# A two-layer vision tower: softmax sums carried by every feature row, a two-part output projection, and row numbers copied by another engine

## The reference, cut to what matters

```
x    = layernorm(h)
q    = rope(x @ Wq) / 4;  kv = rope(x @ Wkv);  v = layernorm per head of kv, * g + b
o    = softmax(q kv^T) v             per image and head; rows 0..997 attend to 0..997,
                                     the last 32 rows to all 1030
h    = h + o_ctx @ Wo_ctx + bo_ctx   for rows 0..997
h    = h + o_lat @ Wo_lat + bo_lat   for the last 32 rows
h    = h + sum over the two best experts of share * swiglu(x_expert)
```

## Time and profile before

| | us |
|---|---|
| median of the timed runs | 4640.12 |
| lowest and highest of 3 | 4629.51, 4647.07 |
| the profiled execution's own time | 4654.99 |
| its span, first to last instruction | 4653.2 |
| stretch of attend | 2178.0 to 3446.6 |
| stretch of project | 3446.6 to 3693.7 |
| stretch of mixture | 4027.2 to 4622.0 |

### The profile page before, as it was taken

The page is one execution under the profiler, slowest core; times in us unless marked ns, Lnnn a source line. Parts: engine busy times, 40 slices in busy tenths (PEclk is TensorE's granted clock), DMA queues, the critical chain, the costliest instruction groups (busy, mean ns, idle before and its releaser), DMA issues. The chain is left out here.

```text
span 4653.2 us, 74405 instructions
## 1 busy us (share of the span) xinstructions
PE 3991.2 (86%) x24046; PEld 2485.3 (53%) x24046; DVE 2531.1 (54%) x4411; ACT 1439.1 (31%) x2890; POOL 1191.6 (26%) x1370
## 2 busy tenths in 40 slices
PE   8799777689999997664999999999957589898885
PEld 8688555557666665442233333333327566666664
DVE  1476369923222222786877777777824454444442
ACT  0122110011111111342577777777741111111110
POOL 0222010034444442464000000000013100177775
PEclk9899897789999998675899999999987699999998
DMA  6122111032333332345233224323239411377776
GB/s 207 49 65 54 40 38 28 25 75 59 61 61 69 70 63 45 105 128 134 42 56 61 47 47 66 50 47 51 48 81 239 106 30 47 88 165 159 162 160 148
DMA packets 335639, 381.02 MB, mean 82 GB/s; under 512 B 44708, under 2 KB 292035, under 8 KB 333823
## 3 DMA queue, kind: packets, MB, share of 16 engines
q1 hardware_dynamic: 255903, 289.46, 25.8%
q0 software_dynamic: 57856, 69.18, 8.7%
q10 hardware_dynamic: 21728, 20.14, 1.5%
HBM read 261.04 MB, written 123.33 MB: 83 GB/s over the span
## 5 line engine op out<-in xcount | busy, mean ns | idle before, releaser
L1931 DVE TENSOR_REDUCE at_mx<-psum 128x1 f32<-128x998 f32 (+1 forms) x768 | 886.4, 1192 | 264.1 <-PE psum L1756 263.5
L1886 ACT ACTIVATE at_p<-psum 128x512 f32<-128x512 f32 (+3 forms) x1536 | 851.5, 588 | 300.1 <-PE psum L1830 270.1
L1830 PE MATMUL psum<-at_q,at_k 99*128 99x512 bf16 (+3 forms) x1536 | 522.1, 383 | 20.3 <-issue 15.2
L1756 PE MATMUL psum<-at_k,at_q 96*128 96x512 bf16 (+3 forms) x1536 | 475.6, 392 | 66.7 <-DMA at_k<-qk_parts 29.3
L1816 PE MATMUL psum<-at_p,at_v 128*32 128x486 f32 (+3 forms) x3072 | 408.3, 604 | 1.0 <-ACT at_p L1886 0.7
L1830 PEld LDWEIGHTS psum<-at_q,at_k 99*128 99x128 bf16 (+1 forms) x1536 | 155.5, 102 | 426.6 <-ACT at_p L1886 273.3
L1173 DVE TENSOR_TENSOR ex_hT<-ex_silu,psum 128x384 f32<-128x384 f32 (+1 forms) x288 | 147.4, 512 | 416.2 <-ACT ex_silu L1142 271.0
L1142 ACT ACTIVATE ex_silu<-psum 128x384 f32<-128x384 f32 (+1 forms) x288 | 131.5, 457 | 776.5 <-PE psum L1086 646.2
L1736 POOL DMA_DIRECT2D o_parts<-at_o x24 | 12.9, 539 | 1247.9 <-DVE at_mx L1931 900.9
L1108 PE MATMUL psum<-ex_wd,ex_hT 128*128 128x192 f32 (+1 forms) x1728 | 291.5, 327 | 0.0
L1756 PEld LDWEIGHTS psum<-at_k,at_q 96*128 96x128 bf16 (+1 forms) x1536 | 152.4, 105 | 229.4 <-DVE at_mx L1931 64.0
(11 more groups left out here) (361 smaller groups left out, 6846.2 us busy)
## 6 DMA issues: line engine op xcount, KB each, us to landing
mx_wd<-in_e_dT SPq DMA_DIRECT2D x72, 288.0 KB, 3.9
qk_parts<-hd_parts SPq DMA_DIRECT2D x32, 579.4 KB, 3.8
at_k<-qk_parts SPq DMA_DIRECT2D x144, 128.8 KB
at_q<-qk_parts SPq DMA_DIRECT2D x144, 124.8 KB
tok_p<-in_x SPq DMA_DIRECT2D x12, 1176.0 KB
mx_wg<-in_e_gT SPq DMA_DIRECT2D x72, 192.0 KB, 2.4
mx_wu<-in_e_uT SPq DMA_DIRECT2D x72, 192.0 KB, 3.4
o_parts<-at_o POOLq DMA_DIRECT2D x24, 515.0 KB
```

The source lines that it names most:

```text
L1756: mm = pe.matmul(psum[0:ctx_rows[t], 3 + 2 * ((PRO + n) % 2) + k, 0:w], Q[v][0:R6, j * 1024 + 128 * t:j * 1024 + 128 * t + ctx_rows[t]], K ...
L1830: pe.matmul(psum[0:n, i % RING, 0:w], K[u][:, j, 128 * t:128 * t + n], Q[u][:, j * 1024 + at:j * 1024 + at + w], start=True, stop=True).th ...
L1886: act.activation(P[0:n, c % 2, j, 0:w], psum[0:n, i % RING, 0:w], ACT.Exp).then_inc(exp_ready, 1)
L1931: dve.tensor_reduce(mx[0:ctx_rows[t], j * CT + t:j * CT + t + 1], pair(n)[0:ctx_rows[t], 0:CTX], AX_X, ALU.max).then_inc(s_free, 1)
```

## The change

Heads sets all 16 columns beside the features of a head to one. The product in attend thus carries the sum 16 times per head, once beside each feature. Attend's store writes 16 feature rows and 16 sum rows of each of the 4 heads as DMAs of their own (8 per unit) into `o_rows`, where features and sums each are 192 rows. The waits on `o_stored` count accordingly.

Project has no reciprocal of all sums at its start and no `recips`. Per image it loads features and sums, each as 128 + 64 partitions, takes two reciprocals (128 and 64 partitions by 1030) and makes two multiplies. PE contracts 128 and then 64 features, 36 matmul records per image. The constants come in 10 DMAs in place of 20, and three memsets fewer stand ahead of them.

Mixture has the copies of row numbers on DVE, as `rows_of` (three chunks ahead, behind `hidden`) and `rows_to` (behind `take_rows`). POOL waits on their semaphores, and for its own carry of four chunks ago.

```diff
...
             pool.memset(eps[:], EPS).then_inc(set_up, 1)
-            pool.memset(v_out[:, :, DH:DH + 1], 1.0).then_inc(set_up, 1)
-            pool.memset(v_out[:, :, DH + 1:HV], 0.0).then_inc(set_up, 1)
+            pool.memset(v_out[:, :, DH:HV], 1.0).then_inc(set_up, 1)
...
         pv_full, o_ready, o_stored = sem("at_pv_full"), sem("at_o_ready"), sem("at_o_stored")
-        LOAD, VLOAD, MROW = 18 * 16, 2 * 16, 3 * 16
+        LOAD, VLOAD, MROW, STORE = 18 * 16, 2 * 16, 3 * 16, 2 * QH * 16
...
-                dst = o_parts[bass.ds(b, 1), u].rearrange("b p n -> (b p) n")
-                pool.dma_start(dst, O[:]).then_inc(o_stored, 16)
+                for j in range(QH):
+                    head = (u * QH + j) * DH
+                    for k in range(2):
+                        dst = o_rows[bass.ds(b, 1), k, head:head + DH].rearrange("b d n -> (b d) n")
+                        pool.dma_start(dst, O[32 * j + DH * k:32 * j + DH * (k + 1), :]).then_inc(o_stored, 16)
...
-                    act.wait_ge(o_stored, g * 16)
+                    act.wait_ge(o_stored, g * STORE)
...
-    LOAD = 16 * 8
-    ZEROED = 8
-    CONSTS = 16 * (2 * (4 + 1) + 2 + 2 * 4)
+    LOAD = 16 * 7
+    ZEROED = 5
+    FEATS = ((0, 128), (128, D - 128))
+    CONSTS = 16 * (2 * (2 + 1) + 4)
     with ExitStack() as ctx:
         sb, sem = names(ctx, nc)
-        wo = sb("pr_wo", [128, 2, QUADS, D])
-        wo_g = sb("pr_wo_g", [128, 2, QUADS, D])
+        wo = sb("pr_wo", [128, 2, 2, D])
...
-        on = sb("pr_on", [128, QUADS, SEQ])
+        op = sb("pr_op", [128, 2, 2, SEQ])
+        sums = sb("pr_sums", [128, 2, 2, SEQ])
+        shares = sb("pr_shares", [128, 2, SEQ])
+        on = sb("pr_on", [128, 2, SEQ])
         hin = sb("pr_hin", [128, 2, NT, D])
...
         def _(sp):
-
-            sp.dma_start(sums[:], o_parts.rearrange("b q (j r) n -> (b q j) r n", r=32)[:, DH, :]).then_inc(sums_in, 16)
-            sp.wait_ge(recip_ready, 1)
-            sp.dma_start(recips.rearrange("b h n -> (b h) n"), shares[:]).then_inc(recip_stored, 16)
-            sp.wait_ge(recip_stored, 16)
             sp.wait_ge(zeroed, ZEROED)
...
                     sp.wait_ge(hb_ready[half], i)
-                    sp.dma_start(op[:, half], o_parts[bass.ds(b, 1)].rearrange("a q p n -> p (a q) n")) \
-                        .then_inc(loaded[half], 16)
-                    for j in range(4):
-                        src = recips.rearrange("b (q j) n -> b j q n", j=4)[bass.ds(b, 1), j]
-                        sp.dma_start(recip[32 * j:32 * j + 32, half], src.broadcast_to([32, QUADS, SEQ])) \
-                            .then_inc(loaded[half], 16)
+                    for k, buf in enumerate((op, sums)):
+                        src = o_rows[bass.ds(b, 1), k].rearrange("a d n -> (a d) n")
+                        for f, (at, n) in enumerate(FEATS):
+                            sp.dma_start(buf[0:n, half, f, :], src[at:at + n]).then_inc(loaded[half], 16)
                     for src, dst in by_tiles(image(h2, b), hin[:, half]):
                         sp.dma_start(dst, src).then_inc(loaded[half], 16)
...
         @block.gpsimd
         def _(pool):
-            for buf in (wo[:], gain[:], shift[:], hin[:], mv[:], xn[:], logits):
+            for buf in (hin[:], mv[:], xn[:], logits):
                 pool.memset(buf, 0.0).then_inc(zeroed, 1)
...
             for n in range(2):
-                for q in range(QUADS):
-                    mm = pe.matmul(psum[:, 5 + n, 0:D], shifts[:], wo[:, n, q, :], start=(q == 0), stop=(q == QUADS - 1))
+                for f, (_, r) in enumerate(FEATS):
+                    mm = pe.matmul(psum[:, 5 + n, 0:D], shifts[0:r, :], wo[0:r, n, f, :], start=(f == 0), stop=(f == 1))
...
                     for t, at, n in tiles:
-                        for q in range(QUADS):
-                            mm = pe.matmul(psum[0:n, k, (t % 2) * D:(t % 2 + 1) * D], on[:, q, at:at + n],
-                                           wo_g[:, int(t == 8), q, :], start=(q == 0), stop=(q == QUADS - 1))
+                        for f, (_, r) in enumerate(FEATS):
+                            mm = pe.matmul(psum[0:n, k, (t % 2) * D:(t % 2 + 1) * D], on[0:r, f, at:at + n],
+                                           wo_g[0:r, int(t == 8), f, :], start=(f == 0), stop=(f == 1))
...
             for n, name in enumerate(("ctx", "lat")):
-                heads = inp[f"L1_attn_Wo_{name}"].rearrange("(q j d) n -> j d q n", j=4, d=DH)
-                for j in range(4):
-                    act.dma_start(wo[32 * j:32 * j + DH, n, :, :], heads[j]).then_inc(consts_in, 16)
-                    head = slice(32 * j, 32 * j + DH)
-                    act.dma_start((gain, shift)[n][head, :], inp[f"L1_attn_ln_{'gb'[n]}"].rearrange("(d a) -> d a", a=1)) \
-                        .then_inc(consts_in, 16)
+                for f, (at, r) in enumerate(FEATS):
+                    act.dma_start(wo[0:r, n, f, :], inp[f"L1_attn_Wo_{name}"][at:at + r]).then_inc(consts_in, 16)
                 act.dma_start(bias[:, n, :], spread(inp[f"L1_attn_bo_{name}"], 128)).then_inc(consts_in, 16)
-            for dst, src in ((ident[:], inp["ident"]), (router[:], inp["routerT"].rearrange("(c p) e -> p c e", c=DC))):
+            for dst, src in ((ident[:], inp["ident"]), (router[:], inp["routerT"].rearrange("(c p) e -> p c e", c=DC)),
+                             (gain[:], inp["pr_gain"]), (shift[:], inp["pr_shift"])):
                 act.dma_start(dst, src).then_inc(consts_in, 16)
...
                 dve.wait_ge(o_full, b * NJ)
-                dve.tensor_tensor(on[:], op[:, half], recip[:, half], ALU.mult).then_inc(scaled[half], 1)
+                for f, (_, r) in enumerate(FEATS):
+                    dve.reciprocal(shares[0:r, f, :], sums[0:r, half, f, :]).then_inc(shares_ready, 1)
+                dve.wait_ge(shares_ready, b * 2 + 2)
+                for f, (_, r) in enumerate(FEATS):
+                    last = dve.tensor_tensor(on[0:r, f, :], op[0:r, half, f, :], shares[0:r, f, :], ALU.mult)
+                last.then_inc(scaled[half], 1)
...
 
-            dve.wait_ge(sums_in, 16)
-            dve.reciprocal(shares[:], sums[:]).then_inc(recip_ready, 1)
             dve.wait_ge(zeroed, ZEROED)
             dve.wait_ge(consts_in, CONSTS)
             dve.tensor_copy(shifts[:], shift[:].to_broadcast([128, 128])).then_inc(shifts_ready, 1)
-            dve.tensor_scalar(wo_g[:], wo[:], gain[:, 0:1], None, ALU.mult).then_inc(wo_ready, 1)
+            for f, (_, r) in enumerate(FEATS):
+                last = dve.tensor_scalar(wo_g[0:r, :, f, :], wo[0:r, :, f, :], gain[0:r, 0:1], None, ALU.mult)
+            last.then_inc(wo_ready, 1)
...
     TURNS = NCH // RING
-    assert TURNS * RING == NCH
+    assert TURNS * RING == NCH and NP == 1
...
         def _(pool):
-            def carry(k):
-
-                pool.tensor_tensor(pad[:, k:k + 1], ident[:, 0:1], ident[:, 0:1], ALU.add)
+            def carry(k, carried):
+
+                pool.tensor_tensor(pad[:, k:k + 1], ident[:, 0:1], ident[:, 0:1], ALU.add).then_inc(carried, 1)
 
             pool.wait_ge(ident_in, 16)
 
             def gather(c, r, again=True):
 
-                pool.tensor_copy(idx[:, r, :], ids[:, bass.ds(c * GS, GS)]).then_inc(idx_ready, 1)
...
                     pool.wait_ge(share_ready, c - RING + 1)
-                carry(4 * r)
+                    pool.wait_ge(gather_carried, c - RING + 1)
+                carry(2 * r, gather_carried)
...
 
-                pool.tensor_copy(to[:, r, :], ids[:, bass.ds(c * GS, GS)]).then_inc(to_ready, 1)
                 pool.wait_ge(to_ready, c + 1)
 
                 pool.wait_ge(added, c * GATHER)
                 for t in range(GS):
                     if t % 2 == 0:
                         pool.wait_ge(ys_ready, c * NP + (t // 2 + 1))
-                        carry(4 * r + 1 + t // 2)
+                        if c is not r:
+                            pool.wait_ge(scatter_carried, c - RING + 1)
+                        carry(2 * r + 1, scatter_carried)
                     pool.indirect_dma_start(y, bass.IndirectOffsetOnAxis(ap=to[:, r, t:t + 1], axis=0),
                                             ys[:, r, t, :], None, compute_op=ALU.add).then_inc(added, 16)
...
         def _(dve):
+            def rows_of(c, r, n_gathered):
+
+                if n_gathered is not None:
+                    dve.wait_ge(gathered[r], n_gathered)
+                here = ids[:, bass.ds(c * GS, GS)]
+                dve.tensor_tensor(idx[:, r, :], here, here, ALU.bitwise_or).then_inc(idx_ready, 1)
+
+            def rows_to(c, r):
+
+                if c is not r:
+                    dve.wait_ge(added, (c - RING + 1) * GATHER)
+                here = ids[:, bass.ds(c * GS, GS)]
+                dve.tensor_tensor(to[:, r, :], here, here, ALU.bitwise_or).then_inc(to_ready, 1)
...
 
-            def step(c, i, r, following=True, before=True):
```

(13 more changed lines are left out.)

26 lines of the change are left out of this document (13 added, 13 removed).

## The result

The changed kernel takes 4687.95 us (4682.7 to 4694.43, 4 runs) against 4643.1 (4629.51 to 4647.07, 4 runs): ratio 1.01, interval 1.0078 to 1.0123. Forecast: 4607, range to 4642.

| stage, us | before | after | difference | forecast |
|---|---|---|---|---|
| attend | 1278.0 | 1285.5 | +7.5 | +4 |
| project | 247.2 | 317.7 | +70.6 | -3 |
| mixture | 601.8 | 564.9 | -36.9 | -34 |
| all others | 2526.0 | 2524.3 | -1.7 | 0 |

A forecast was written before the change was run, and what follows sets the result against it. It took transfers to bound project and POOL's scatters, gathers and issue time to bound mixture. Mixture -34, project -3 and attend +4 sum to -33 us, from a median of 4640 to 4607 us, range 4578 to 4642.

The forecast's parts named there:

- The failed step: Project: a third of the projection matmuls goes, so an image's 54 in 11.13 us become 36 in 7.4.
- project term: Project stage as a whole: -3 us, from pace +6, start -1 and tail -8; bounds -20 and +98.
- The pace: Project, image to image: scale 15.6, PE's projection 7.5, last hout add out at 8.2; 23.8 us against 23.0 before.
- Rival 3: Project: slower, reciprocals stay uncovered because DVE waits for late stores; 98 us at most, 4708 us; chance 0.13.
- The collision: Project: POOL's bias add holds DVE's reciprocals as it held the multiply; 32 us more, taken as 0; chance 0.05.
- Start and tail: Project: first projection at 36.6 us against 37.7, -1; tail -8, with the last projection 3.8 shorter.
- Mixture: Mixture: copies leave POOL, the other chain bounds; chunk 7.24 + 0.22 for rows_of = 7.46, before 7.97; gain 34 us.
- the pad's 0.41: Mixture: what remains for pad and gap before each gather and scatter on POOL, 0.41 us each; bounds 0.34 and 0.94.
- rival 1: Mixture: the scatter's landing takes the place of the copies, chunk 8.0, no gain, 4640 us; chance 0.14.
- Rivals 1, 2 and 4: The last, in mixture: POOL's queue doesn't run ahead, keeps 0.5 us issue stalls; gain 19, 4622 us; chance 0.12.
- rival 2: Mixture: row numbers hide in DVE's queue, chunk 7.24, -52; project -12; sum -60, 4580 us; chance 0.16.
- Attend: End of attend: eight store DMAs per unit in place of one cost +4 us, bounds 0 and +7.

The follow-up runs named there:

- e5: The changed kernel with the 64-row part filled up with zeros, so that PE contracts 128 rows there too: 4620.57 us, 0.9964 of before.
- e10: The changed kernel with the next image's reciprocals moved ahead of the adds that wait for this image's projection: 4639.55 us, 1.0007 of before.
- e6: e4 without the two reciprocals of an image, multiplying by the sums (another output): 4559.81 us, 0.9829 of before.
- e4: The changed kernel with features as 96 + 96 in place of 128 + 64: 4626.1 us, 0.9947 of before.
- e9: The changed kernel with 96 + 96 features, one attend store per unit, rows_of behind the xT copies, and one reciprocal for all images: 4566.39 us, 0.9855 of before.

## Why the prediction was wrong

**The failed step** is "a third of the projection matmuls (54 in 11.13 us become 36 in 7.4)". It priced by count and took the mean of a uniform sequence for an alternating one. Measured: 16.52 us, 9.1 more in each of eight images, 73 us, as much as the whole miss (forecast -33, spans +39.5). e5 shows that the count alone would have been near, 8.24 at equal heights, in a stage of 251.8 for the 244 forecast. So 66 of the 73.6 us of the project term go with the alternation, and the other 8 are smaller misses of pace and start that e5 has too. The rise of the clock within a projection, on which 11.13 rested, was an assumption never named: spacings of 0.32 and then 0.16 us stand inside that one row of x54.

**The missed row** was in the trace of before, in the mixture: the weight loader's stall where 128 rows are followed by 64, at the full clock. The prediction could have priced the stall from it (17 changes of 0.33 us are 5.6 us an image), but not the clock that stays low.

```profile
4301.15 0.41 PEld L2748 LDWEIGHTS psum<-mx_xT,mx_wu 128*128 128x128 f32 x2
4301.89 0.18 PEld L2752 LDWEIGHTS psum<-mx_xT,mx_wr 64*128 64x128 f32 x1 [0.33 <-issue]
```

The Trainium skill's page "TensorE: Matmul & The Clock Gate" (section "Step-by-step: what each phase is for") has PE pull weight loads ahead of running matmuls where row groups don't conflict or the load goes to the background buffer. The trace agrees for equal heights (0.32 and 0.16 us, no gap) and not for alternating ones; which of the two conditions fails there no run shows.

**The pace.** Its form was right: 15.6 (13.1 + 2.4 + 0.1) + projection + 0.7 in one line, and e10 shows that it is one line. With 16.5 for 7.5 the same sum gives 32.8; measured 32.4. At equal heights it is 24.4 for the 23.8 forecast. "A pace over 27 us proves the forecast wrong there" did its work, but the sign had another cause than the rival's.

**Rival 3** had the sign and the place (project, DVE waits) and another mechanism: stores that land late. Those waits went, so its sign is no merit of its reasoning. What it says of the reciprocals is half true: 64 of 104 us were exposed (e6), but in a stage that would have ended level (e4, 248.4 for 247.2).

**The collision** did not come: reciprocals took 6.5 us throughout, beside POOL's bias add (3.42 us) as well. By the rule of "GPSIMD Engine Reference", section "8. Key points", of the Trainium skill, one-input reciprocals should be free of it; the trace agrees: in each of the eight images one of the two lies beside the add and takes 6.52 to 6.58 us, as the other does. Where a multiply and the add meet, one of the two can be held: in e9 a multiply took up to 5.12 us for 1.2, while in the kernel before three of them kept their 3.4 us and the add took up to 6.55 for 3.42.

**Start and tail.** First projection 40.8 us into the stage, forecast 36.6. The bias was 4 us later than the forecast 21:

```profile
3476.58 0.56 DVE L2231 TENSOR_TENSOR pr_bias<-psum,pr_bias 128x384 f32<-128x384 f32 x1 [3.32 <-PE psum L2107]
```

From the start of the last projection to the stage's end it is 44.2 us before (from 3649.51) and 50.3 after (from 3719.16): +6 for the forecast -8. With equal heights it is 38 (e5), 6 less than before. Of the stage's +70.6 us, 3 are the start, 61 the seven paces and 6 the tail.

**Mixture** was right in sum (-36.9 for -34) and mechanism: POOL's copies went, and the other chain bounds. That the chunk came within 0.01 (7.45 for 7.46) is in part luck. rows_of was put at 0.22 us on 7.24; the start of hot_share moved by 0.21 in the chunk shown, but moving rows_of away bought only 0.10 a chunk and left 7.35. So one term was too high and the other too low, and whether the 0.1 above 7.24 is rows_to, or rows_of in its new place, no run shows. POOL's scatter kept its 0.51 us, so the pad's 0.41 was too low there, without cost. The 3.15 us landing of rival 1 does hold the pad up (0.56 us), off the path. Rivals 1, 2 and 4 fell. The -12 that rival 2 gives project is not worked out: the tail's -8 was in the -3 already.

**Attend**: +5.3 at its end for +4; the rest of the +7.5 is within the stage's scatter.

## What to carry to other kernels

A matmul's price is that of its place in a sequence: before splitting a contraction unevenly, look for a row where two heights follow each other, and prefer equal parts, or padding with zeros. Where two engines take turns, any price on either is paid in full, so first ask whether the order can put them side by side. And when a term scales a measured total, ask what clock that total ran at, and whether the new sequence still earns it.

## What the runs showed of the hardware

- Products of 128 and 64 contracted rows in turn: 0.46 to 0.48 us a record (192 columns, fp32, two records a product) for 0.32 at 1.2 GHz, 0.26 for 0.16 at 2.4 GHz.
- 36 alternating records in 16.5 us left the clock at 1.2 GHz; 36 of equal height, after the same idle time, saw it rise on the way (8.24 us). PE with 28.12 busy of 28.90 us stayed at 1.2 GHz too (e10).
- Fewer and in part smaller matmuls took longer than more: 36 in 16.52 us, 54 in 11.13.
- A DVE reciprocal of 1030 columns takes 6.5 us on 64, 96 and 128 partitions alike, a multiply of that length 1.2.
- Eight stores of 16 rows behind one another ahead of a stage's end cost 5.3 us more than one of 128 rows: 3.3 of it their issue (3.81 us for 0.53), 2.0 the longer time from there to the next stage (7.90 us for 5.86).
